# Row sums ahead of the first residual's transposes, and the third norm and the division by row sums right behind that residual, in a loop over 32 token tiles

## The reference

```python
def reference(x, ctx, ...):
    x = x + wkv(w, u, k=layernorm(x), v=ctx)            # exp-weighted running mean over 128 time steps, per channel
    x = x + attention(layernorm(x), Wa, Wp, w_std, w_rec)   # 16 heads of 32, causal softmax, @ Wp
    x = x + mlstm(q=layernorm(x), k=ctx, v=ctx, Wi, bi, Wf, bf, ln_scale)
    x = x + experts(layernorm(x), gate_w, w_gate, w_up, w_down)
    return x

def mlstm(...):
    log_f_cum = cumsum(log_sigmoid(fg)); log_D = causal(log_f_cum[s] - log_f_cum[t] + ig[t])
    D = exp(log_D - max_t log_D)
    C = (q @ k.T) / sqrt(32) * D
    h = C / (max(|C.sum(-1)|, exp(-max log_D)) + 1e-6) @ v     # then a norm per head, times ln_scale

def experts(x, ...):                                    # x: 4096 tokens
    w, sel = top_k(softmax(x @ gate_w), 8)
    pos = running count of each expert's tokens          # pairs with pos >= 2048 are dropped
    out[t] += w * (silu(xg @ w_gate) * (xg @ w_up)) @ w_down
```

## Time and profile before

| | |
|---|---|
| median of 3 runs | 2272.83 us (2267.55 to 2279.23) |
| profiled execution | 2280.1 us, span of its instructions 2278.3 us |
| busy: TensorE, its weight load | 2008.4 us (88%), 1459.6 us (64%) |
| busy: VectorE, ScalarE, GpSimd | 1581.6 us (69%), 1203.3 us (53%), 1534.6 us (67%) |
| HBM | 133.07 MB read, 96.73 MB written, 101 GB/s over the span |
| mean granted TensorE clock | 0.964 of full speed |

### The profile page before, as it was taken

How to read it: one execution, slowest core, us unless ns; L and a number is a source line. 1 busy time by engine, 2 the same in 40 slices (tenths; PEclk the granted TensorE clock), 3 DMA queues, 4 the chain that set the end, 5 groups by cost and what they waited for, 6 DMA issues and landing times. The chain is left out here.

```text
span 2278.3 us, 66587 instructions
## 1 busy us (share of the span) xinstructions
PE 2008.4 (88%) x22279; PEld 1459.6 (64%) x22280; DVE 1581.6 (69%) x3262; ACT 1203.3 (53%) x3018; POOL 1534.6 (67%) x1622
## 2 busy tenths in 40 slices
PE   2899999999899899998748999999999999999986
PEld 2676666666666666666426776676776777767664
DVE  6688877877777777876445775777666667666663
ACT  3576556566656655665424554555454445554542
POOL 4247766766766776776667777777776777776764
PEclk9999999999999999999869999999999999999998
DMA  3111001001101000001028787777887878786874
GB/s 118 44 39 39 28 28 37 28 28 37 30 25 37 31 29 33 33 28 40 20 59 175 165 183 157 166 166 155 177 170 165 165 166 179 166 169 134 180 143 79
DMA packets 136030, 219.47 MB, mean 96 GB/s; under 512 B 28032, under 2 KB 61184, under 8 KB 135936
## 3 DMA queue, kind: packets, MB, share of 16 engines
q0 software_dynamic: 73472, 139.82, 32.0%
q1 hardware_dynamic: 57856, 70.17, 9.8%
q10 hardware_dynamic: 4608, 8.39, 1.0%
HBM read 133.07 MB, written 96.73 MB: 101 GB/s over the span
## 5 line engine op out<-in xcount | busy, mean ns | idle before, releaser
L2268 POOL DMA_INDIRECT out_dram<-y,m_add x300 | 498.4, 1661 | 218.1 <-POOLq L2276 156.4
L2418 PE MATMUL ps<-xh,wh 128*128 128x256 f16 (+1 forms) x1752 | 381.4, 267 | 6.4 <-PEq L2430 4.7
L2419 PE MATMUL ps<-xh,wl 128*128 128x256 f16 (+1 forms) x1752 | 381.4, 267 | 1.6 <-issue 1.6
L557 POOL DMA_INDIRECT slot_scratch<-pair,slots x248 | 295.0, 1190 | 79.2 <-issue 55.8
L2260 POOL DMA_INDIRECT xg<-z_scratch,slot_t x260 | 264.5, 1017 | 84.6 <-issue 75.6
L2499 ACT ACTIVATE y<-ps,wts_now 128x512 f32<-128x512 f32 x294 | 185.5, 682 | 148.0 <-ACTq L2498 123.5
L2423 PE MATMUL ps<-xl,wh 128*128 128x256 f16 (+1 forms) x1752 | 229.0, 267 | 2.5 <-PEq L2434 2.0
L2573 DVE SCALAR_TENSOR_TENSOR hx<-ps,s 64x256 f16<-64x256 f32 x146 | 62.2, 426 | 235.4 <-issue 131.1
L2418 PEld LDWEIGHTS ps<-xh,wh 128*128 128x128 f16 x1752 | 171.8, 98 | 52.8 <-issue 24.3
L2515 ACT ACTIVATE xh<-ps 128x512 f16<-128x512 f32 x146 | 87.2, 597 | 217.6 <-ACTq L2514 184.8
L2419 PEld LDWEIGHTS ps<-xh,wl 128*128 128x128 f16 x1752 | 171.8, 98 | 29.4 <-issue 0.8
(11 more groups left out here) (342 smaller groups left out, 5165.3 us busy)
## 6 DMA issues: line engine op xcount, KB each, us to landing
wst<-in_L_ffn_w_gate_dram SPq DMA_DIRECT2D x32, 384.0 KB
wst<-in_L_ffn_w_up_dram SPq DMA_DIRECT2D x32, 384.0 KB
xt<-in_x_dram SPq DMA_DIRECT2D x32, 256.0 KB
ct<-in_ctx_dram SPq DMA_DIRECT2D x32, 256.0 KB, 2.6
out_dram<-x SPq DMA_DIRECT2D x32, 256.0 KB
z_scratch<-zn ACTq DMA_DIRECT2D x32, 256.0 KB, 2.0
wdst<-in_L_ffn_w_down_dram SPq DMA_DIRECT2D x32, 256.0 KB
out_dram<-y,m_add POOLq DMA_INDIRECT x300
```

The lines of the kernel that those rows point to most:

```text
L557: pool.indirect_dma_start(out=slot_d[:, :], out_offset=bass.IndirectOffsetOnAxis(ap=slots[:, k:k + 1], axis=0), in_=pair[:, k, :], in_offs ...
L2268: pool.indirect_dma_start(out=acc_d[:, :], out_offset=bass.IndirectOffsetOnAxis(ap=m_add[:, k, h:h + 1], axis=0), in_=y[:, k, h, :], in_of ...
L2418: pe.matmul(ps[:, dst, 0:cols], wh[:, j, k, c0:c0 + P], xh[:, k, 0:cols], start=(k == 0), stop=False)
L2419: pe.matmul(ps[:, dst, 0:cols], wl[:, j, k, c0:c0 + P], xh[:, k, 0:cols], start=False, stop=False)
```

## The change

On TensorE the masks of banks 0, 1 and 3 are issued behind a wait for a new semaphore of q_copy, and the mask of bank 2 behind the wait for k_copy, as before; head_norm is waited for ahead of both. row_sums moves ahead of y_turn. take_places_ready, which releases GpSimd's make_keys, is now raised by TensorE when it passes its wait for places_taken.

On ScalarE q_copy moves behind head_rstd. On VectorE head_norm moves ahead of mark_best, and weighted_ctx behind it; take_places is split: the copy moves ahead of denominator_error and add_past_ctx, and the sum (count_chosen) behind wkv_ratio, with a semaphore that choose of the next step waits for; and behind the first residual the order becomes third_norm, best_keys, division by row sums, key_matches, stats1 with the release of the x load, matched_weights.

```diff
@@ ScalarE, step @@
                         query_norm().then_inc(query_norm_ready, 1)
-                    if on(1):
-                        act.wait_ge(q_ps, 1)
-                        act.sem_inc(q_ps, -1)
-                        q_copy()
                     if on(3):
                         act.wait_ge(head_var_ready, 1)
...
                         head_rstd().then_inc(head_rstd_ready, 1)
+                    if on(1):
+                        act.wait_ge(q_ps, 1)
+                        act.sem_inc(q_ps, -1)
+                        q_copy().then_inc(q_copy_ready, 1)
@@ TensorE @@
+                def score_masks(banks):
+                    for r in banks:
+                        for q_ in range(4):
+                            i = slice(32 * ((q_ + r) % 4), 32 * ((q_ + r) % 4) + 32)
+                            pe.matmul(ps[32 * q_:32 * q_ + 32, S_BANK + r, :], identb[i, i],
+                                      mask_ts[i, r, :].unsqueeze(1).to_broadcast([32, 4, T]),
+                                      start=True, stop=False, skip_group_check=True)
+
                 def scores():
-                    masks(S_BANK, mask_ts)
...
                         query_turn().then_inc(query_turn_ps, 1)
-                    if on(1):
-                        pe.wait_ge(k_copy_ready, 1)
-                        pe.sem_inc(k_copy_ready, -1)
                     if on(3):
                         pe.wait_ge(head_norm_ready, 1)
                         pe.sem_inc(head_norm_ready, -1)
                         if at != nb + 2:
                             pe.sem_inc(head_norm_ready_for_pool, 1)
                     if on(1):
+                        pe.wait_ge(q_copy_ready, 1)
+                        pe.sem_inc(q_copy_ready, -1)
+                        score_masks((0, 1, 3))
+                        pe.wait_ge(k_copy_ready, 1)
+                        pe.sem_inc(k_copy_ready, -1)
+                        score_masks((K_BANK - S_BANK,))
                         scores().then_inc(scores_ps, 1)
...
                     if on(4):
                         pe.wait_ge(places_taken, 1)
                         pe.sem_inc(places_taken, -1)
+                        if at not in (nb + 2, nb + 3, nb + 4):
+                            pe.sem_inc(take_places_ready, 1)
                     if on(1):
                         v().then_inc(v_ps, 1)
+                    if on(1):
+                        pe.wait_ge(exps1_ready, 1)
+                        pe.sem_inc(exps1_ready, -1)
+                        pe.wait_ge(exps0_ready, 1)
+                        pe.sem_inc(exps0_ready, -1)
+                        row_sums().then_inc(row_sums_ps, 1)
                     if on(0):
                         pe.wait_ge(wkv_ratio_ready, 1)
                         pe.sem_inc(wkv_ratio_ready, -1)
-                    if on(1):
-                        pe.wait_ge(exps1_ready, 1)
-                        pe.sem_inc(exps1_ready, -1)
-                    if on(0):
                         y_turn().then_inc(y_turn_ps, 1)
                     if on(1):
-                        pe.wait_ge(exps0_ready, 1)
-                        pe.sem_inc(exps0_ready, -1)
-                        row_sums().then_inc(row_sums_ps, 1)
@@ VectorE @@
                 def take_places():
-                    dve.tensor_copy(pos[:, :], ps[:, PL_BANK, 0:E]).then_inc(take_places_ready, 1)
+                    return dve.tensor_copy(pos[:, :], ps[:, PL_BANK, 0:E])
+
+                def count_chosen():
                     return dve.tensor_tensor(selacc[:, :], selacc[:, :], selb[:, :], ALU.add)
...
                         best_eight().then_inc(dve_step, 1)
-                    if on(0):
-                        weighted_ctx().then_inc(dve_step, 1)
+                    if on(3):
+                        dve.wait_ge(head_rstd_ready, 1)
+                        dve.sem_inc(head_rstd_ready, -1)
+                        head_norm().then_inc(head_norm_ready, 1)
                     if on(4):
...
                         mark_best().then_inc(dve_step2, 1)
-                    if on(3):
-                        dve.wait_ge(head_rstd_ready, 1)
-                        dve.sem_inc(head_rstd_ready, -1)
-                        head_norm().then_inc(head_norm_ready, 1)
+                    if on(0):
+                        weighted_ctx().then_inc(dve_step, 1)
+                    if on(5):
+                        dve.wait_ge(counted, 1)
+                        dve.sem_inc(counted, -1)
...
                         row_max().then_inc(row_max_ready, 1)
...
+                    if on(4):
+                        dve.wait_ge(places_ps, 1)
+                        dve.sem_inc(places_ps, -1)
+                        take_places().then_inc(places_taken, 1)
                     if on(0):
...
                         add_past_ctx()
...
-                    if on(4):
-                        dve.wait_ge(places_ps, 1)
-                        dve.sem_inc(places_ps, -1)
-                        take_places().then_inc(places_taken, 1)
...
                         wkv_ratio().then_inc(wkv_ratio_ready, 1)
+                    if on(4):
+                        count_chosen().then_inc(counted, 1)
...
                         first_residual().then_inc(first_residual_ready, 1)
-                    if on(4):
-                        dve.wait_ge(make_keys_ready, 1)
-                        dve.sem_inc(make_keys_ready, -1)
-                        best_keys().then_inc(dve_step, 1)
-                    if on(0):
-                        dve.wait_ge(first_residual_ready, 1)
-                        dve.sem_inc(first_residual_ready, -1)
-                        dve.sem_inc(first_residual_ready_for_sp, 1)
-                        stats1().then_inc(dve_step, 1)
...
                         third_norm().then_inc(third_norm_ready, 1)
                     if on(4):
-                        dve.wait_ge(dve_step, 1)
-                        dve.sem_inc(dve_step, -1)
-                        key_matches().then_inc(dve_step2, 1)
+                        dve.wait_ge(make_keys_ready, 1)
+                        dve.sem_inc(make_keys_ready, -1)
+                        best_keys().then_inc(dve_step, 1)
...
                         divide_by_row_sums().then_inc(divide_by_row_sums_ready, 1)
+                    if on(4):
+                        dve.wait_ge(dve_step, 1)
+                        dve.sem_inc(dve_step, -1)
+                        key_matches().then_inc(dve_step2, 1)
+                    if on(0):
+                        dve.wait_ge(first_residual_ready, 1)
+                        dve.sem_inc(first_residual_ready, -1)
+                        dve.sem_inc(first_residual_ready_for_sp, 1)
+                        stats1().then_inc(dve_step, 1)
```

5 lines of the change are left out of this document (added).

## The result

The changed kernel is slower: 2327.47 us in the median (2326.63 to 2329.8) against 2276.03 us for the kernel before on the same chip, a ratio of 1.0231 (95% interval 1.0206 to 1.0256). The forecast was 2241.5; the sign was wrong. The profiled execution has a span of 2328.0 us, 49.7 more than before.

What follows compares the result with a forecast made beforehand. No engine was full; waits in the token-tile loop set its step (scores behind the k copy, GpSimd's keys, log_d behind Rt). Gains 20.8 + 2.4 + 8.3 = 31.5 us gave 2241.5; range 2229 to 2258, eight in ten 2218 to 2272.

Steps and rivals of the forecast that it cites:

- Nothing is lost: VectorE behind the residual: later x load lets the projection start at 623.1, wanted at 623.74; no cost, 0.65 us spare.
- rival C: Late x load, released behind more VectorE waits, delays the projection by 0.65 us a step: 2293 us; chance 0.18.
- The masks: TensorE before the scores: three banks' masks ahead of the k copy, scores 0.24 us behind it; gain 0.6 a step.
- up to 0.7 comes back to GpSimd: GpSimd's store beside the scan, 1.88 us long, others near 1.0: shorter if the scan comes later, else nothing gained.
- The rule weighed: VectorE with two SBUF inputs and GpSimd reading SBUF exclude each other; weighted_ctx beside cc would wait 1.1 us, sum unchanged.
- take_places: Earlier copy of the places: GpSimd's make_keys starts 0.4 to 1.4 us earlier, 0.8 taken, x being the last input.
- The first residual: Behind row_sums and y_turn, put at 617.1, 0.25 us later than now, with v at 612.75.
- The steps before step 6: Steps 2 to 5, places missing or new: only the scores' part counted, 4 x 0.6 = 2.4 us gained.
- The clock: Five more of 26 loop steps escape a fall of the clock worth 1.66 us each: 8.3 us gained.
- The sum of 0.8 us a step: All parts together in one loop step, over steps 6 to 31: 26 x 0.8 = 20.8 us gained.

Runs made afterwards that it cites:

- e5: The changed kernel with three of GpSimd's indirect pair stores moved from behind Rt to behind hold_ctx of the next step: 2303.93 us, ratio 1.0072.
- e1: The changed kernel with the first-residual wait and the release of the x load back right behind the first residual: 2300.73 us, ratio 1.0088.
- e2: The changed kernel with VectorE's old order behind the first residual, row sums still ahead of the residual's transposes: 2293.64 us, ratio 1.0058.
- e3: The changed kernel with the first residual's transposes ahead of row sums again, VectorE's new order kept: 2296.72 us, ratio 1.0070.
- e4: The changed kernel with both old orders around the first residual; masks, q copy, head_norm and early copy of places stay changed: 2280.11 us, ratio 1.0004.
- e14: The changed kernel, late release included, with four stores moved as in e8: 2257.26 us, ratio 0.9888.
- e8: e4 with three stores moved from behind Rt to behind hold_ctx and one beside the scores moved behind scale_heads: 2214.47 us, ratio 0.9667.
- e10: e8 with the release of the x load moved from ahead of stats1 to behind the divide: 2262.9 us, ratio 0.9885.
- e6: The kernel before with only three stores moved from behind Rt to behind hold_ctx of the next step: 2233.06 us, ratio 0.9754.
- e9: e1 with the four stores moved as in e8: 2245.31 us, ratio 0.9814.
- e12: e8 with the first of the three stores put back behind Rt: 2181.98 us, ratio 0.9520.
- e13: The kernel before with the stores placed as in e12 and nothing of the change: 2184.09 us, ratio 0.9573.
- e15: e12 with one GpSimd product of 128x8 ahead of the store left behind Rt: 2183.09 us, ratio 0.9551.
- e11: e8 with three unread GpSimd products of 128x340 behind Rt, in the old place of the three stores: 2255.1 us, ratio 0.9840.

## Why the prediction was wrong, point by point

- The structure of the loss. Three pieces meet. (1) Row sums ahead of the transposes put weighted_v and GpSimd's work earlier than the first residual: Rt starts 0.70 before it (547.41) where it was 0.73 behind it, so the first store of the tail starts at 0.50, 0.72 into weighted_v. (2) That holds weighted_v up by 1.5 us (divide at 2.76 against 1.23 in e5). (3) The x load hangs on the divide, and so does stats0, which VectorE takes behind it. With the load alone freed (e1) the projection stays where it was; with (3) wholly away (e2) or (2) away (e3) the loss is 0.4 to 0.5 us a step over e4, most of it in falls, with both 1.84. With four stores moved the same orders cost 1.17 (e14 against e8), more than half of it in falls. These are differences of single profiled executions, good to a few tenths.
- "New: 618.9 + 4.0 = 622.9 ... Nothing is lost". This is the step that failed. I took the divide at 1.5 behind the residual, by the inverse; it came at 2.76, by weighted_v. The price of what follows was right: 4.46 from the load to the projection, 4.2 in rival C. In the prediction's own times the load left at 617.1 + 3.25 = 620.35, past its point of 619.5. Rival C had the place and the sign, and the load as the link; it was given 0.18 and 0.65 us a step, and the loss is 1.55. It had neither the held-up burst, nor VectorE's order as a second way to the same wait, nor the long falls.
- The masks. Scores start 0.46 behind the k copy (535.35) where I had 0.24: a gain of 0.39 rather than 0.6. It was then lost twice over, as row_max starts 1.3 later behind the scores. The cause is a gain that the prediction itself names: the store beside the scan shrank from 1.88 to 1.24 (535.53), so the next one starts 1.27 behind the scores and no longer 1.57. I had booked it as "up to 0.7 comes back to GpSimd".
- The rule weighed. weighted_ctx took 1.88 beside cc, as the rule of the Trainium skill has it (SBUF — State Buffer, section Who interferes with whom), and cv 0.67 in its new place. That part was right, and it cost what was said. What I missed is that the wait moved on: denominator_error (540.89) took 1.52 beside GpSimd's x, where it had taken 0.69.
- take_places. The copy came early (540.79), but its signal left TensorE only with minus_max (542.61), and GpSimd was idle 1.41 between x (ended 541.85) and its keys (543.26). I had x as the last input; it was the signal. From minus_max to the keys it is 0.65, before 1.07: 0.4 gained, the lower end of my bounds. No row shows the 0.6 us by which I let the signal run ahead of the matmuls; the keys started 0.35 ahead of v, which leaves less than that.
- The first residual. From v to the residual 4.50 us, forecast 4.35, before 3.46. y_turn 0.99 behind row_sums (forecast 0.88). Right within 0.15.
- The steps before step 6 were to gain 2.4 and lost 14.5. In e10 the late load alone costs 10.6 there over e8; that the tiles that fill the pipeline have no other stage to hide it is my explanation, not a test.
- The clock. I let five more steps escape; two more did, but nine falls got twice as long. In e6 to e9, e12, e13 and e15 the projection starts 5.35 to 5.92 us behind the residual, and there are none in these 25 steps; in e1 to e5, e10 and e14, where it mostly starts at 6.2 to 8.0, there are ten to 24 (e11, at 5.9 to 6.7, has four, in the q product). The fall's price, 1.66 for a short one, held (33.67 to 35.25 is 1.6).
- The forecast gain. The sum of 0.8 us a step would have been 0.1 to 0.3 without any collision (e13). I priced each start against the latest input that the trace showed and took the gain whole. That another chain closes the circle behind it is argued, not shown. In the last subtraction 2248.6 less 7.3 is 2241.3, not 2241.5; nothing hangs on it.

What stays open: by which path a store holds TensorE (not by the loading of instructions, as far as the profile shows: between 233.4 and 1124.1 us that of the changed kernel has no packet in the instruction queues); what sets its size, since stores at the same place make the divide 2.98 behind weighted_v in the changed kernel and 3.7 in e1 and e2, in steps of some 0.7; why a store 0.97 behind weighted_v holds it in one step of e4 and not in another; why the store at 551.26 shows in a qk that starts 0.56 later, while one in e12 leaves a log_d that starts 0.61 later alone; and how the orders' own 0.9 us a step are made up.

## What to carry to other kernels

When a part of an order moves, list every transfer that another engine issues within the next microseconds and ask what it will now start beside; a queue that wins time can collide with what it used to miss. Look for rows of TensorE with idle time put down to "issue" inside a burst, and for a consumer whose wait is longer in the loop than in the first steps, where a stage is still missing: both showed the hold-up in the kernel before; moving four stores was worth 4.3% there (e13), twice what the change cost. When a wait has two ways to it, free both before judging one (e1 against e2), and count the falls of the clock apart: half of several differences here was falls. And keep the release of a load off any wait that it doesn't need.

## What the runs showed of the hardware that I had not expected

An indirect store that GpSimd starts while TensorE has a burst of small-tile matmuls in hand delays this burst: 0.57 us for one store into weighted_v (e12), 1.53 for one 0.72 into it (changed kernel against e5), 1.4 for one into the scores (e4, 2.80, against e8, 1.43), 0.7 between the pieces of qk, and 2.2 from log_d to the exp with the stores of the kernel before (3.85, against 1.62 in e6). A start 0.94 us or more behind weighted_v cost nothing in e3, e12, e13 and e15, though the store lasts another microsecond; in e4 starts of up to 0.97 still did. That the small tiles matter is by contrast alone, not by a test of its own: the projection's f16 matmuls of 128x128 tiles keep their 0.21 through a store's start (e6). They differ from the bursts in type and in how many start in a microsecond as well, and no run parts these. Three GpSimd products over the whole of log_d left it at most 0.5 us late (e11).

SBUF — State Buffer of the Trainium skill, section Who interferes with whom, says "PE and ACT never wait on anyone." and that a DMA never contends with a compute engine. Both sentences are about the ports of SBUF, and no run here shows where a store holds TensorE, at a port or elsewhere. Taken as a promise that TensorE keeps its time beside a store of GpSimd, they don't hold in these runs; the measurement decides.
